# Row gathers of a routed mixture layer issued one at a time, one block later, each behind VectorE's product

## The reference

```python
for j in range(2):                       # two layers, same weights, own router
    gate = xf @ router_W[j] + router_b[j]
    _, ids = top_k(gate + gate_bias[j], 2)               # 2 of 6 experts for each token
    weights = softmax(where(sel, gate, -inf))
    h = xf @ exp_Wup[e] + exp_bup[e]
    h = silu(h @ exp_Wg[e] + exp_bg[e]) * h
    eo = h @ exp_Wdown[e] + exp_bdown[e]
    combined = einsum('ne,enh->nh', weights, eo)
    y = xf + combined + share_out        # share_out: two shared experts on every token
    xf = y * rsqrt(mean(y * y) + eps) * norm_w[j]
```

## Time and profile before

| | us |
|---|---|
| median of 3 runs | 2671.09 |
| the three runs | 2663.04, 2671.09, 2671.52 |
| the profiled execution, in all | 2655.1 |
| its span | 2653.1 |
| TensorE busy | 2456.7 (93%) |
| VectorE busy | 1927.3 (73%) |
| ScalarE busy | 1574.4 (59%) |
| GpSimd (POOL) busy | 462.5 (17%) |
| the 128 gathers L1768 on POOL | 125.3 busy, 979 ns each in the mean |

### The profile page before, as it was taken

The page is one execution under the profiler, slowest core; times in us unless marked ns, Lnnn a source line. Parts: engine busy times, 40 slices in busy tenths (PEclk is TensorE's granted clock), DMA queues, the critical chain, the costliest instruction groups (busy, mean ns, idle before and its releaser), DMA issues. The chain is left out here.

```text
span 2653.1 us, 55050 instructions
## 1 busy us (share of the span) xinstructions
PE 2456.7 (93%) x20198; PEld 1487.9 (56%) x20198; DVE 1927.3 (73%) x3194; ACT 1574.4 (59%) x3344; POOL 462.5 (17%) x534
## 2 busy tenths in 40 slices
PE   6886999999999999999999999988999999998897
PEld 6775444444444444444444444477788877787785
DVE  8766888888888888888888888566533644544557
ACT  4441577777777777777777777843244433442442
POOL 2001100101010101010010101022332423422514
PEclk9897899999999999999999999987999999999998
DMA  7999674756566564747465654242134322422533
GB/s 255 395 363 289 90 106 77 96 84 85 91 79 89 80 96 65 104 65 95 81 89 87 82 86 69 55 154 98 57 121 127 116 70 78 120 68 68 170 102 104
DMA packets 163778, 305.66 MB, mean 115 GB/s; under 512 B 44455, under 2 KB 111150, under 8 KB 155182
## 3 DMA queue, kind: packets, MB, share of 16 engines
q1 hardware_dynamic: 150174, 265.53, 48.1%
q0 software_dynamic: 12288, 33.57, 4.0%
q10 hardware_dynamic: 1072, 3.23, 0.5%
HBM read 165.10 MB, written 127.68 MB: 110 GB/s over the span
## 5 line engine op out<-in xcount | busy, mean ns | idle before, releaser
L811 ACT ACTIVATE at_P<-at_ST 128x512 f32<-128x512 f32 (+4 forms) x2176 | 1095.9, 559 | 372.5 <-PE at_ST L854 350.3
L762 DVE TENSOR_REDUCE f_part<-at_R 128x2 f32<-128x804 f32 x1024 | 976.0, 994 | 121.4 <-PE at_R L842 117.0
L869 PE MATMUL at_OP<-at_P,at_V 128*32 128x256 f32 x8192 | 642.0, 385 | 16.0 <-ACT at_O L819 12.9
L854 PE MATMUL at_ST<-at_Q,at_K 64*128 64x512 f32 (+4 forms) x1428 | 343.7, 455 | 3.5 <-ACT at_P L811 3.5
L869 PEld LDWEIGHTS at_OP<-at_P,at_V 128*32 128x32 f32 x8192 | 163.3, 108 | 264.2 <-ACT at_P L811 185.7
L842 PE MATMUL at_R<-at_K,at_Q 64*128 64x402 f32 x1344 | 271.2, 392 | 5.1 <-DVE f_part L762 5.1
L745 POOL TENSOR_SCALAR_AFFINE_SELECT at_P<-at_P 128x512 f32<-128x512 f32 x128 | 81.6, 637 | 1089.1 <-ACT at_P L811 1089.1
L854 PEld LDWEIGHTS at_ST<-at_Q,at_K 64*128 64x128 f32 (+1 forms) x1428 | 141.6, 180 | 218.5 <-ACT at_P L811 203.6
L759 DVE TENSOR_REDUCE f_mx<-at_R 128x2 f32<-128x256 f32 (+3 forms) x256 | 209.9, 821 | 42.8 <-PE at_R L835 40.7
L1825 DVE TENSOR_TENSOR ex_ab<-ex_bank,ex_sg 128x256 f32<-128x256 f32 x148 | 62.8, 424 | 226.1 <-ACT ex_sg L1908 167.4
L842 PEld LDWEIGHTS at_R<-at_K,at_Q 64*128 64x128 f32 x1344 | 128.0, 185 | 115.8 <-issue 69.2
(11 more groups left out here) (246 smaller groups left out, 4170.3 us busy)
## 6 DMA issues: line engine op xcount, KB each, us to landing
at_K<-k_parts SPq DMA_DIRECT2D x126, 264.1 KB, 9.2
k_parts<-pj_kpart SPq DMA_DIRECT2D x32, 800.5 KB, 8.5
expert_rows<-ex_rb SPq DMA_DIRECT2D x148, 128.0 KB
ex_xb<-sorted SPq DMA_DIRECT2D x72, 256.0 KB
v_items<-pj_vbuf SPq DMA_DIRECT2D x32, 544.0 KB, 8.0
q_parts<-pj_qpart SPq DMA_DIRECT2D x32, 512.0 KB, 10.6
at_Q<-q_parts SPq DMA_DIRECT2D x252, 64.0 KB, 9.6
f_K<-k_parts SPq DMA_DIRECT2D x60, 264.1 KB, 9.9
```

What stands on the lines that cost most here:

```text
L762: dve.tensor_reduce(part[:, :, p, q, c], buf[:, :, 0:XC], AX.X, ALU.max).then_inc(s_drain, 1)
L811: act.activation(Pt[(NKT * n + s) % NP][0:rows, h, c0:T], ST[(NST * n + s * G + h) % NB][0:rows, c0:T], ACT.Exp, scale=SCALE).then_inc(s_e ...
L854: pe.matmul(ST[t % NB][0:rows, c0:T], K[n % NU][half, p, keys], Q[n % NU][half, kind, p, c0:T], start=True, stop=True).then_inc(s_st, 1)
L869: ins = pe.matmul(OP[32 * h:32 * h + 2 * D, at], V[n % 2][0:rows, key_tile(s), h, :], Pt[(NKT * n + s) % NP][0:rows, h, at], start=s in (0 ...
```

## The change

It does three things to GA. Each gather becomes an event of its own, (GA, r, t, j). In the three stretches among routed blocks, the two gathers of tile t, which both stood at slot 0 of block k0+t, now stand at slot 0 and slot 3 of block k0+t+1; in the last section the second gather of a tile stands one event later than the first. And `pace` holds for them too: each waits on `s_a` for the product in front of it. The combines keep their places.

```diff
--- before.py
+++ after.py
@@ -1555,7 +1555,8 @@
 
             l = r // NHF
             for t in range(HT):
-                at(k0 + t, 0, ("GA", r, t))
+                at(k0 + t + 1, 0, ("GA", r, t, 0))
+                at(k0 + t + 1, 3, ("GA", r, t, 1))
                 at(k0 + t + 3, 1, ("E1", r, t))
                 at(k0 + t + 3, 2, ("E2", r, t))
                 at(k0 + t + 4, 1, ("ES", r, t))
@@ -1629,7 +1630,7 @@
         def after(i, *ev):
             then.setdefault(i, []).extend(ev)
 
-        events += [("GA", r, t) for t in range(NGB)]
+        events += [("GA", r, t, j) for t in range(NGB) for j in range(2)]
         i = -1
         dense, sums = shared_events(r)
         for i, e in enumerate(dense + sums):
@@ -1637,8 +1638,8 @@
             if e[0] == "S":
                 t = QT * passes[e[1]][1] + e[2]
                 after(i, ("E1", r, t))
-                after(i + 1, ("E2", r, t), *([("GA", r, t + NGB)] if t + NGB < HT else []))
-                after(i + 2, ("ES", r, t))
+                after(i + 1, ("E2", r, t), *([("GA", r, t + NGB, 0)] if t + NGB < HT else []))
+                after(i + 2, ("ES", r, t), *([("GA", r, t + NGB, 1)] if t + NGB < HT else []))
                 if t % QT == QT - 1:
                     g = t // QT
                     after(i + 3, ("EM", r, g), ("EP", r, g))
@@ -1658,13 +1659,13 @@
         use, dno, tno = number("U", "UP"), number("S", "DNE"), number("T")
         sno, gno, acno = number("S"), number("G"), number("AC")
         eno, emno, eono = number("E1"), number("EM"), number("EO")
-        assert list(eno) == [("E1",) + e[1:] for e in number("E2")] == [("E1",) + e[1:] for e in number("GA")]
+        assert list(eno) == [("E1",) + e[1:] for e in number("E2")] == [("E1",) + e[1:3] for e in number("GA") if e[3] == 0]
 
         pace, taken = {}, 0
         for e in events:
             if e in use:
                 taken = use[e] + 1
-            elif e[0] == "SC" and taken:
+            elif e[0] in ("SC", "GA") and taken:
                 pace[e] = taken
         upc, ups = {}, 0
         for e in use:
@@ -1757,17 +1758,18 @@
                             pool.wait_ge(s_a, pace[e])
                         R.scatter(pool, *e[1:], XS, XR)
                     elif e[0] == "GA":
-                        r, t, n = e[1], e[2], eno["E1", e[1], e[2]]
+                        r, t, j, n = e[1], e[2], e[3], eno["E1", e[1], e[2]]
                         h = r % NHF
-                        if t == 0:
+                        if t == 0 and j == 0:
                             for u in range(NX3):
                                 pool.wait_ge(s_rs[u], 16 * len([k for k in range(NBK * (r + 1)) if k % NX3 == u]))
-                        if n >= NGB:
+                        if n >= NGB and j == 0:
                             pool.wait_ge(s_e2, n - NGB + 1)
-                        for j in range(2):
-                            pool.indirect_dma_start(gb[n % NGB][j][:, :], None, RS[h],
-                                                    bass.IndirectOffsetOnAxis(ap=R.IDX[h][:, j, t:t + 1], axis=0)
-                                                    ).then_inc(s_ga[n % NGB], 16)
+                        if e in pace:
+                            pool.wait_ge(s_a, pace[e])
+                        pool.indirect_dma_start(gb[n % NGB][j][:, :], None, RS[h],
+                                                bass.IndirectOffsetOnAxis(ap=R.IDX[h][:, j, t:t + 1], axis=0)
+                                                ).then_inc(s_ga[n % NGB], 16)
                     elif e[0] == "EP":
                         n = emno["EM", e[1], e[2]]
                         pool.wait_ge(s_ms, n + 1)
```

## The result

The change takes **2647.97 us** in the median of four runs (2645.80 to 2648.93); before took 2667.64 (2663.04 to 2671.52) beside it. The ratio is **0.9928, with a 95% interval of 0.9911 to 0.9946**: 0.72% faster. Forecast were 0.55% and 2656 us, with a range of 2638 to 2670.

What follows compares the result with a forecast made beforehand. TensorE, busy 2456.7 of 2653.1 us, bounds the kernel; gather stretches lose 35.9 us. Burst -17.7 plus residual 3.0, other terms 0, gives -14.7 us: 2656 us against the 2671.09 median, range 2638 to 2670.

Steps and rivals of the forecast that it cites:

- (b): First four blocks of each gather stretch: gathers in pairs instead of eight in a row win 17.7 us, less 3.0 staying.
- (c): Rest of the three stretches, already at two gathers a block: 18.2 us lost there stay, change 0, bounds -9.1 and +1.5.
- (d): VectorE's combines E1 do not wait for the later gathers: 3.2 us slack, 1.1 us once in four tiles; cost 0.
- (e): Last section, four passes of dense work: holding back a tile's second gather costs 0, bounded by +1.25 us.
- Rival 1: In the stretches, two gathers a block are themselves too dense, so the lag comes some blocks later: 2668 us, chance 0.20.
- Rival 2: In the stretches, the wait cures all lags, since a late product gives POOL a rest: -33 us, 2638 us, chance 0.12.
- Rival 3: POOL falls behind at the power and runs without rest through the stretches: +8 us, 2679 us, chance 0.05.
- Rival 4: Gathers beside VectorE's combines E1 and E2 block each other 0.95 us a block: +12 us, 2683 us, chance 0.03.

Runs made afterwards that it cites:

- slower pace: The change with the third stretch's 16 tiles at every 1.75th block instead of every block, combines, powers and norms too, on chip B: 2602.02 us, ratio 1.0015 to before.

## Why the prediction was right

The sign, the size and the place came out: -19.7 us between the medians beside a forecast of -15, and faster by over 0.3% had a chance of 0.69. In part the size is luck: two terms were off and nearly cancel. The burst gave 17.2 us instead of the 14.7 that were counted on, and the rest of the stretches, beside the same profile of before, gave back 3.3 of them, so the stretches are 14.0 us shorter. Point by point:

- **The burst** (b). 17.7 us were to be won less 3.0 that stay; 17.2 were won, so only 0.4 to 0.5 stayed. The lag behind the second pairs is there (Silus 3.37 us apart instead of 2.88), and TensorE, a block ahead, did not feel it. The wait alone, at the old place, does the same (0.8 us left of 15.0 on chip A), and so this step is shown by an experiment. In that kernel all four blocks have gathers.
- **The spread rest** (c) was taken as unchanged, with bounds of -9.1 and +1.5. It came out at +3.3 in the profile, outside the bound. The step took it that the rest runs at two gathers a block, in before and in the change. It does not: in before, rows of four to six gathers stand around the powers, and there lie its largest lags outside the bursts (3.4 to 4.1 us). POOL gets behind at each power and each late product, and what it does with the backlog decides. Single profiles differ by some us, though: the second profile of before loses 22.7 us in the rest (37.7 less 15.0), more than the 21.5 of the change, and on chip C the rest lost 19.6 us in the change (6.6 + 7.9 + 6.1 less 1.0) and 21.5 in before (38.0 less 16.5), so only "about unchanged" can be said.
- **But the move alone was a cost that the working did not have.** The order shown for the power (three gathers that stood in front of it now stand behind) was read for the slack of E1 only. Its real price was in (c): without the wait, 17 us more are lost. In the change the wait keeps this from happening, and no run shows that the move gives anything: the wait alone gains as much. Of the rivals, 3 named this place, a power in front of gathers that must catch up; what it missed is that the wait itself breaks up the row.
- **Slack of E1** (d). Predicted cost 0. One combine waited for its gather, 0.2 us in all.
- **The last section** (e) was bounded by +1.25 us and was 93.03 us instead of 92.05, +1.0; the second profile of before has 93.4, so the +1.0 is within what two profiles differ by. On chip B, where nothing is late, it is up to +2.8; part of that may be the slower pace's norms, which end later there. The last power had 0.2 us before the norm that needs it; now the norm idles for it and starts 0.03 us after its end (2637.87 + 1.01, and 2638.91).

- **The rivals.** Rival 1 (pace no cure) falls with the first four blocks, which lose 0 to 0.4 us, though it was right that the pace leaves a lag: 21.5 us are still lost at it. That the lag is made by the recording falls with the medians: runs without a profile gained too. Rival 2 (a cure for all) falls with 21.9 us still lost. Rival 3 did not come. Rival 4, gathers blocked by combines, falls with 956 ns, 477 and 476 ns in the median: the Trainium skill's rule in "SBUF — State Buffer", "Who interferes with whom", on VectorE with two SBUF inputs is not seen in these rows, in which 61 of the 128 gathers run at the same time as a combine (46 in before). The rule "issue early" of "DMA: Bandwidth & Descriptors", "Rules for kernel authors", of the Trainium skill, would have had the wait bring nothing. Here a wait that issues later, alone, brings 0.67%, and a later place without a wait costs 0.71%; it is not early or late that decides, but how many go in a row, in these kernels.
- **What no rival had** is that it all hangs on the chip. Three of the chips A to D showed the lag. The change was not run on B; its first two stretches stand in the slower-pace kernel there word for word and take 60.55 us, as those of before do, and its last section would be up to 2.8 us longer. From that it should be even or 0.1% slower there. That is worked out, not measured.

## What to carry to other kernels

Read who waits for "remote", and what another engine does over and over at that time: here indirect DMAs in a row on GpSimd made TensorE's completions come 3 to 6 us late at ScalarE, with no row that named them. A wait of each gather for some product of the running work shortens such rows of gathers. It cost nothing in the stretches; what it costs in the last section is at most the 2.8 us of chip B, and is hidden on A and C by what single profiles differ by. It does not bound the rows by itself: where POOL is behind its waits, as behind a power on chip B, eight still go out together. Scatters in a row deserve the same look; nothing was tried on them here. Look also at what may hold the gathers' queue back (a power, a late buffer), since everything behind it then goes out at once. And time such a change on more than one chip before you give its gain a number: it was 0.7%, 0.4% and, by what the stretches of another kernel show, nothing.

## What the runs showed of the hardware

- Indirect gathers issued by GpSimd without a rest (0.95 us each, 0.30 apart) delay what other engines see of TensorE's ends: from 0.47 us to between 2.7 and 6.6 us in rows of seven or eight, and to at most 2.8 us in the change's stretches, where no more than four stand together on one side of a power. Plain DMAs of the same size from the same queue (0.54 us each) do not, nor do those of SP. Indirect scatters in a row (0.96 us each, 0.30 apart) stand beside waits of VectorE of 4.7 and 4.3 us on chip A, where chip B has 1.5 us and none; no run varied them.
- It happened on chips A, C and D and not on B, where gathers in a row took the same time to issue. Before takes 2667, 2655 and 2661 us on the three, and 2598 on B.
- The lag costs more than itself: the clock falls to 0.81 to 0.90 of full in the mean of the four blocks behind the burst, and stays at 1.00 in the same blocks wherever the lag is gone.
